# Sixteen shift numbers transposed at once and laid out as two rows by a DMA

## The chip, the cores and the metric

The kernel runs on one core of a Trainium2 chip. The metric is the device time of one execution, in microseconds (us). Five engines work side by side, each on its own program in order, and wait for one another on semaphores: TensorE (PE: matmuls, and PEld for loading its stationary operand), VectorE (DVE), ScalarE (ACT), GpSimd (POOL) and SyncE (SP), which here issues nearly all DMAs.

## The reference, cut to what matters

Two layers run one behind the other on eight sequences (the batches below) of 512 rows and 512 features: a graph attention, and then a transformer block. The change lies in the attention of the second. Shortened:

```
h = gamma * layernorm(hidden) + beta            # [8, 512, 512]
q, k, v = split(h @ Wqkv.T + bqkv)              # 16 heads of 32
energy = q @ k.T                                # per head [512, 512]
att = softmax(energy, axis=-1) / sqrt(512)
out = (att @ v) @ Wp.T + bp
h1 = out + hidden
y = gamma * layernorm(h1) + beta + h1
```

The softmax needs, for each query row, a number that is subtracted before the exponential: the row's maximum.

## The kernel before, in words

The function `attention` goes through 8 batches of 8 pairs of heads (`batch`, p from 0 to 7), 64 pairs in all. The heads' q and k are held as sums of a high and a low part, and are stacked for one matmul: `sq_stack` and `sk_stack` (`sq`, `sk`) have in rows 0 to 95 the three products' parts, and in rows 96 and 97 `sq` has the shift, in two parts (high and low), while `sk` has ones. So the matmul of 98 rows gives energy minus maximum at once.

For a pair, PE makes the energies twice. `scores` (L1351, 8 tiles of 128 queries by 512 keys, two heads by NT = 4 tiles) is for the maxima alone: DVE reduces each tile (`maximum`, L1167) into `mx`, and `shift_parts` (L1175, L1177) makes the 16 negated numbers per partition in `shift` (2 heads, 4 tiles, 2 parts). `shift_t` turns them from columns into rows on PE, by matmuls against the identity (L1359), into PSUM; ACT copies the rows into `sq` (`shift_rows`, L1058). `scores_t` (L1375) then makes the transposed energies with the shift, ACT takes the exponential (`exps`, L1067, into `pt`), and `weighted` multiplies with v and with ones (L1389, L1391).

This is staggered over pairs: while pair p goes through `scores_t`, `exps` and `weighted`, the `scores` of the next pair run between them, and `shift_t` of the next pair stands near the end of the pair. Behind it, and ahead of the next pair's `scores_t`, PE has filling work written out by hand: half a projection of 6 matmuls (L48 to L50) behind most pairs, 30 matmuls at p = 1, 18 at p = 4, and at p = 0 only the pair's last `weighted`. In the first and the last batch some of the filling is missing: p = 2 of the first and p = 4 of the last have only their `weighted` too. Where a pair has half a projection there, its last `weighted` is held back until behind the next pair's first `scores_t`.

SP issues the DMAs in the order of its own program: `stacks` copies a chunk of q and k (two pairs) from `qh`, `ql`, `kh`, `kl` into the stacks by 24 DMAs of 64 KB (L930), and stands at the head of each even p; `load_t` stands in p = 1, `store_y` and `load_h` in p = 7, where SP waits for the last piece of the batch before. A chunk's 24 DMAs are asked for one or two pairs before they are used. Batches 0, 1, 2 and 7 stand in the program by themselves; 3 to 6 are a loop of two passes with two batches each.

Below, T0 to T7 are the moments at which the `shift_t` *for* pair 0 to 7 of a batch begins (T0 falls in the pair p = 7 of the batch before, T1 in p = 0). The lag of a pair is the time from its T to its first `scores_t`.

Of the kernel before, what the change touches and what calls it, by code (L numbers as in the profile page):

```python
# [16 lines left out]
F32 = mybir.dt.float32  # L17
# [6 lines left out]
P = 128  # L24
# [789 lines left out]
def attention(nc, t, d):  # L814
# [12 lines left out]
    with ExitStack() as ctx:  # L827
        def sb(name, shape, dt=F32):
# [17 lines left out]
        mx = sb("mx2", [P, 2, NT, 2])  # L846
        shift = sb("shift", [P, NT, 2, 2], F32R)
# [5 lines left out]
                          "k_ready qh_done ql_done kh_done kl_done e_ready emax_done sh_hi sh_lo sh_ready shrow_done "  # L853
                          "et_ready exp_done pv_done den_done oraw_done rden_done o_done oh_done ol_done v_ready v_done "
                          "pj_ready hb_done h1_done st_done mv_done ve_done rstd_done nmr_done ln_done mulg_done "
                          "addb_done y_done y_out")
# [43 lines left out]
        def _(sp):  # L900
# [31 lines left out]

            def batch(b, bpar, more):
                for p in range(PAIRS):
                    c = p // 2
                    if p % 2 == 0 and (c < 3 or more):
                        stacks((c + 1) % FC, 4 * b + c + 2)
                    if p == 1 and more:
                        sp.wait_ge(s["hl_done"], 4 * b + 4)
                        load_t(b + 1)  # L940
                    if p == 7:
                        if first(b):
                            load_h(b)
                        else:
                            sp.wait_ge(s["y_done"], 4 * b)
                            store_y(b - 1)
                            load_h(b)

# [6 lines left out]
            stacks(0, 1)  # L955
            batches(sp, batch)
# [72 lines left out]
        def _(act):  # L1029
# [24 lines left out]
            def shift_rows(b, p):  # L1054

                for k in range(2):
                    act.wait_ge(s["sh_ready"], 2 * (PAIRS * b + p) + k + 1)
                    nc.scalar.activation(sq[3 * DH:3 * DH + 2, (p // 2) % 2, 2 * (p % 2) + k, :],  # L1058
                                         bank[3 * DH:3 * DH + 2, 2 + k, :], ACT.Copy).then_inc(s["shrow_done"], 1)
# [94 lines left out]
        def _(dve):  # L1154
# [8 lines left out]
            def maximum(b, p, i):  # L1163

                dve.wait_ge(s["e_ready"], 8 * (PAIRS * b + p) + i + 1)
                k, n = divmod(i, NT)
                nc.vector.reduce_max(mx[:, p % 2, n, k:k + 1], bank[:, 2 + i % 2, :], AX).then_inc(s["emax_done"], 1)  # L1167

            def shift_parts(b, p):

                G = PAIRS * b + p
                dve.wait_ge(s["emax_done"], 8 * G + 8)
                if not (isinstance(b, int) and G == 0):
                    dve.wait_ge(s["sh_ready"], 2 * G)
                nc.vector.tensor_scalar(shift[:, :, :, 0], mx[:, p % 2], -1.0, None, ALU.mult).then_inc(s["sh_hi"], 1)  # L1175
                dve.wait_ge(s["sh_hi"], G + 1)
                nc.vector.scalar_tensor_tensor(shift[:, :, :, 1], mx[:, p % 2], -1.0, shift[:, :, :, 0].bitcast(F32),  # L1177
                                               ALU.mult, ALU.subtract).then_inc(s["sh_lo"], 1)
# [112 lines left out]
        def _(pe):  # L1291
# [44 lines left out]
            def scores(b, p, i):  # L1336
# [3 lines left out]
                if i == 0:  # L1340
                    pe.wait_ge(stq[c % 2][p % 2], STK * (use(b, c) + 1))
                    pe.wait_ge(stk[c % 2][p % 2], STK * (use(b, c) + 1))
                    if not (isinstance(b, int) and G == 0):
                        pe.wait_ge(s["shrow_done"], 2 * G)
# [9 lines left out]
            def shift_t(b, p):  # L1354

                pe.wait_ge(s["sh_lo"], PAIRS * b + p + 1)
                for k in range(2):
                    for n in range(NT):
                        last = nc.tensor.matmul(bank[3 * DH:3 * DH + 2, 2 + k, n * P:(n + 1) * P],  # L1359
                                                shift[:, n, k, :].bitcast(F32), t["ident"][:, :],  # L1360
                                                start=True, stop=True)
                    last.then_inc(s["sh_ready"], 1)

            def scores_t(b, p, i):
# [3 lines left out]
                for k in range(2):  # L1368
                    if i == 0:
                        pe.wait_ge(s["shrow_done"], 2 * G + k + 1)  # L1370
# [230 lines left out]
```

## Time and profile before

| | |
|---|---|
| time before, median of 3 runs | 1713.22 us (1706.87 to 1714.64) |
| the profiled execution: span from the first to the last instruction | 1703.8 us |
| time of the profiled execution beside its span | the page states the span alone; the runs lie 3.1 to 10.8 us above it |
| PE busy | 1563.1 us, 92% |
| DVE, ACT, POOL busy | 58%, 43%, 23% |
| first and last `shift_t` | 636.8 and 1655.1 us |
| matmuls of `shift_t` | 1024 instructions, 125.1 us |
| ACT copies of the shift rows | 128, 75.5 us |

A busy share is an average over the span. What a change is worth is read from which wait ends last at its place.

### The profile page before, as it was taken

Reading aid. Unit: us, or ns where it says so; the run is one execution under the profiler, and the core shown is the slowest. Engines: PE = TensorE matmul, PEld = TensorE weight load, DVE = VectorE, ACT = ScalarE, POOL = GpSimd, SP = SyncE. Lnnn points to the kernel's source line nnn. Section 1 sums busy time; section 2 is a strip of 40 time slices with the busy share of each in tenths; the row PEclk is TensorE's granted clock in tenths of the full one; section 3 lists DMA queues with packets and bytes.
Section 4 is the critical chain, followed back from the end, with each engine's and each line's share of the span. In section 5 each row is a group of like instructions: output and inputs, shape, how many; then the busy total and the mean of one; then the engine's idle time right before and its main releaser. Section 6 shows DMA issues by size and latency. Waiting matters only on the chain.

```text
span 1703.8 us, 22572 instructions
## 1 busy us (share of the span) xinstructions
PE 1563.1 (92%) x7716; PEld 927.4 (54%) x7716; DVE 984.3 (58%) x1454; ACT 726.9 (43%) x1249; POOL 394.3 (23%) x265
## 2 busy tenths in 40 slices
PE   6979899999997279999999999999998999999993
PEld 4646566666665254555555555555554554654542
DVE  2533567666676335556556565665655666566665
ACT  0231334234341325554554554554454455465361
POOL 1023344333432040110140140140131131032032
PEclk9989999999998689999999999999999999999997
DMA  9454133342322432122133133133132124123112
GB/s 293 171 179 131 53 126 128 134 150 79 128 85 75 175 90 72 48 85 81 39 112 86 38 109 90 38 109 84 44 98 75 47 57 133 38 62 104 45 41 74
DMA packets 97180, 162.24 MB, mean 95 GB/s; under 512 B 39104, under 2 KB 47616, under 8 KB 90928
## 3 DMA queue, kind: packets, MB, share of 16 engines
q1 hardware_dynamic: 95920, 160.44, 30.6%
q8 instruction: 62, 1.02, 0.3%
q10 hardware_dynamic: 1152, 0.41, 0.1%
q14 instruction: 46, 0.38, 0.1%
HBM read 72.67 MB, written 37.78 MB: 65 GB/s over the span
## 4 chain that ended last, share of the span: by engine, by line
PE 58%; DVE 5%; issue 1%; ACT 1%; POOL 1%; DMA 1%; SPq 0%; DVEq 0%; ACTq 0%; POOLq 0%
PE a_bank L1389 13%; PE a_bank L1351 9%; PE a_bank L48 8%; PE a_bank L1359 7%; PE a_bank L49 7%; PE a_bank L50 7%; PE a_bank L1375 7%; DVE mx L1167 3%; DVE shift L1175 1%; PE a_bank L1391 1%; DMA traw<-t_rows 1%; POOL hl L968 0%; ACT pt L1067 0%; DVE o L1189 0%; DVE rden L1184 0%
## 5 line engine op out<-in xcount | busy, mean ns | idle before, releaser
L1167 DVE TENSOR_REDUCE mx<-a_bank 128x1 f32<-128x512 f32 x512 | 339.9, 687 | 256.6 <-PE a_bank L1351 252.1
L1067 ACT ACTIVATE pt<-a_bank 128x512 f32<-128x512 f32 x512 | 277.3, 595 | 151.4 <-PE a_bank L1375 148.3
L1391 PE MATMUL a_bank<-pt,ones 128*32 128x512 f32 x1024 | 276.3, 606 | 0.0
L1389 PE MATMUL a_bank<-pt,v 128*32 128x512 f32 x1024 | 272.3, 606 | 0.0
L1351 PE MATMUL a_bank<-sk_stack,sq_stack 96*128 96x512 f32 x512 | 206.9, 445 | 5.5 <-DVE mx L1167 2.1
L1351 PEld LDWEIGHTS a_bank<-sk_stack,sq_stack 96*128 96x128 f32 x512 | 88.0, 188 | 186.7 <-DVE mx L1167 135.0
L1375 PE MATMUL a_bank<-sq_stack,sk_stack 98*128 98x512 f32 x512 | 169.0, 406 | 2.5 <-ACT pt L1067 1.7
L1058 ACT ACTIVATE sq_stack<-a_bank 2x512 fp32r<-2x512 f32 x128 | 75.5, 590 | 206.4 <-PE a_bank L1359 206.4
L740 PE MATMUL g_bank<-m,sf 128*128 128x320 f32 x512 | 155.2, 446 | 1.9 <-issue 1.9
L1359 PE MATMUL a_bank<-ident,shift 128*2 128x128 f32 x1024 | 125.1, 276 | 13.2 <-DVE shift L1177 13.2
L48 PE MATMUL a_bank<-hh,wqkh 128*128 128x512 f32 x256 | 107.8, 421 | 25.8 <-POOL hl L968 25.0
L978 POOL TENSOR_TENSOR rstd<-ve,mhalf 128x4 f32<-128x4 f32 x8 | 8.1, 1018 | 495.3 <-DVE ve L1220 495.3
L1375 PEld LDWEIGHTS a_bank<-sq_stack,sk_stack 98*128 98x128 f32 x512 | 96.3, 190 | 44.0 <-ACT pt L1067 15.5
L1359 PEld LDWEIGHTS a_bank<-ident,shift 128*2 128x2 f32 x1024 | 82.8, 86 | 66.2 <-DVE shift L1177 34.9
L740 PEld LDWEIGHTS g_bank<-m,sf 128*128 128x128 f32 x512 | 93.4, 191 | 41.7 <-issue 11.1
L1184 DVE RECIPROCAL rden<-den 128x512 f32<-128x512 f32 x32 | 107.2, 3350 | 5.4 <-ACT den L1076 5.4
L49 PE MATMUL a_bank<-hl,wqkh 128*128 128x512 f32 x256 | 101.3, 396 | 0.0
L50 PE MATMUL a_bank<-hh,wqkl 128*128 128x512 f32 x256 | 100.9, 394 | 0.0
L1159 DVE SCALAR_TENSOR_TENSOR kl<-a_bank,bcol,kh 128x512 fp32r<-128x512 f32 x32 | 24.0, 750 | 115.6 <-ACT kh L1045 115.6
L48 PEld LDWEIGHTS a_bank<-hh,wqkh 128*128 128x128 f32 x256 | 48.6, 190 | 66.2 <-issue 58.3
L1389 PEld LDWEIGHTS a_bank<-pt,v 128*32 128x32 f32 x1024 | 39.1, 108 | 83.2 <-issue 78.4
L490 POOL TENSOR_TENSOR e<-e,cadd 128x640 f32<-128x640 f32 x32 | 49.5, 1547 | 130.1 <-DVE e L633 128.6
(164 smaller groups left out, 2606.2 us busy)
## 6 DMA issues: line engine op xcount, KB each, us to landing
sq_stack<-qh SPq DMA_DIRECT2D x256, 64.0 KB, 2.0
sk_stack<-kh SPq DMA_DIRECT2D x256, 64.0 KB, 2.0
m_rows<-mout SPq DMA_DIRECT2D x8, 1280.0 KB, 5.0
m<-m_rows SPq DMA_DIRECT2D x8, 1280.0 KB, 5.6
xraw<-in_x_t SPq DMA_DIRECT2D x8, 1024.0 KB, 7.7
xn<-in_x SPq DMA_DIRECT2D x8, 1024.0 KB, 5.0
h_rows<-xn SPq DMA_DIRECT2D x8, 1024.0 KB, 4.0
t_rows<-hout SPq DMA_DIRECT2D x8, 1024.0 KB, 3.9
```

Of the source, the lines that this page charges most:

```text
L48: nc.tensor.matmul(out, ah, bh, start=start, stop=False)
L49: nc.tensor.matmul(out, ah, bl, start=False, stop=False)
L50: return nc.tensor.matmul(out, al, bh, start=False, stop=stop)
L740: nc.tensor.matmul(out, sf2[:, par, f, i * P:(i + 1) * P], m[:, f, dr, :], start=f == 0, stop=False)
L1067: nc.scalar.activation(pt[:, i, k, :], bank[:, k, :], ACT.Exp).then_inc(s["exp_done"], 1)
L1167: nc.vector.reduce_max(mx[:, p % 2, n, k:k + 1], bank[:, 2 + i % 2, :], AX).then_inc(s["emax_done"], 1)
L1184: nc.vector.reciprocal(rden[:, :], den[:, :]).then_inc(s["rden_done"], 1)
L1351: nc.tensor.matmul(bank[:, 2 + i % 2, :], sq[0:3 * DH, c % 2, j, n * P:(n + 1) * P], sk[0:3 * DH, c % 2, j, :], start=True, stop=True).the ...
L1359: last = nc.tensor.matmul(bank[3 * DH:3 * DH + 2, 2 + k, n * P:(n + 1) * P], shift[:, n, k, :].bitcast(F32), t["ident"][:, :], start=True, ...
L1375: nc.tensor.matmul(bank[:, k, :], sk[0:3 * DH + 2, c % 2, j, i * P:(i + 1) * P], sq[0:3 * DH + 2, c % 2, j, :], start=True, stop=True).the ...
L1389: nc.tensor.matmul(bank[a:a + DH, 4 + p % 2, :], v[:, bpar, i, (2 * p + k) * DH:(2 * p + k + 1) * DH], w, start=i == 0, stop=i == NT - 1)
L1391: last = nc.tensor.matmul(bank[r:r + DH, 4 + p % 2, :], ones32[:, :], w, start=i == 0, stop=i == NT - 1)
```

## The change

`shift` is stored with part and head outermost, so that one transpose on PE turns the whole [128, 16] block into [16, 128] (one instruction instead of eight matmuls in the program). ACT copies these 16 short rows of 128 numbers from PSUM into a new SBUF tile `sht`. A DMA that SP issues then lays them out as the two rows of 2 x 512 numbers in `sq`. `scores_t` waits for that DMA (`shrow_in`), the next pair's `scores` for the copy (`sht_done`). On SP the new `shift_rows` stands at the end of each pair's piece of the program, behind `stacks`, `load_t` or `load_h`.

```
-        mx = sb("mx2", [P, 2, NT, 2])
-        shift = sb("shift", [P, NT, 2, 2], F32R)
+        mx = sb("mx2", [P, 2, 2, NT])
+        shift = sb("shift", [P, 2, 2, NT], F32R)
+        sht = sb("sht", [4 * NT, P])
...
         @block.sync
+            def shift_rows(b, p):
+                G = PAIRS * b + p
+                sp.wait_ge(s["sht_done"], G + 1)
+                sp.dma_start(sq[3 * DH:3 * DH + 2, (p // 2) % 2, 2 * (p % 2):2 * (p % 2) + 2, :].bitcast(F32)
+                             .rearrange("o k (n c) -> o (k n) c", c=P), sht[:, :]).then_inc(s["shrow_in"], 16)
...
                             load_h(b)
+                    if next_pair(b, p, more):
+                        shift_rows(*next_pair(b, p, more))
...
             sp.wait_ge(s["set_up"], 4)
             stacks(0, 1)
+            shift_rows(0, 0)
...
         @block.scalar
             def shift_rows(b, p):
-                for k in range(2):
-                    act.wait_ge(s["sh_ready"], 2 * (PAIRS * b + p) + k + 1)
-                    nc.scalar.activation(sq[3 * DH:3 * DH + 2, (p // 2) % 2, 2 * (p % 2) + k, :],
-                                         bank[3 * DH:3 * DH + 2, 2 + k, :], ACT.Copy).then_inc(s["shrow_done"], 1)
+                G = PAIRS * b + p
+                act.wait_ge(s["sh_ready"], G + 1)
+                if not (isinstance(b, int) and G == 0):
+                    act.wait_ge(s["shrow_in"], 16 * G)
+                nc.scalar.activation(sht[:, :], bank[0:4 * NT, 2, 0:P], ACT.Copy).then_inc(s["sht_done"], 1)
...
         @block.tensor
             def shift_t(b, p):
                 pe.wait_ge(s["sh_lo"], PAIRS * b + p + 1)
-                for k in range(2):
-                    for n in range(NT):
-                        last = nc.tensor.matmul(bank[3 * DH:3 * DH + 2, 2 + k, n * P:(n + 1) * P],
-                                                shift[:, n, k, :].bitcast(F32), t["ident"][:, :],
-                                                start=True, stop=True)
-                    last.then_inc(s["sh_ready"], 1)
+                nc.tensor.transpose(bank[0:4 * NT, 2, 0:P], shift[:, :, :, :].rearrange("p e k n -> p (e k n)").bitcast(F32),
+                                    t["ident"][:, :]).then_inc(s["sh_ready"], 1)
...
             def scores_t(b, p, i):
                     if i == 0:
-                        pe.wait_ge(s["shrow_done"], 2 * G + k + 1)
+                        pe.wait_ge(s["shrow_in"], 16 * G + 16)
                         pe.wait_ge(s["exp_done"], 8 * G)
```

In the program of SP, this is the end of one batch and the beginning of the next in the program before: the loads of p = 7 (L908, L909), the 24 DMAs of `stacks` of p = 0, `load_t` of p = 1 (L905), and the first of the next `stacks`.

```order
231 L908 DMA h<-h_rows 128x2048
232 L909 DMA rows<-gb_rows 128x1024
233 L930 DMA sq_stack<-qh 32x512 [waits qh_done]
234 L930 DMA sq_stack<-qh 32x512 x3
...
237 L930 DMA sk_stack<-kh 32x512 [waits kh_done]
238 L930 DMA sk_stack<-kh 32x512 x3
...
243 L930 DMA sk_stack<-kh 32x512 x4
244 L930 DMA sk_stack<-kl 32x512 x2
245 L905 DMA traw<-t_rows 128x2048 [waits hl_done]
246 L930 DMA sq_stack<-qh 32x512 [waits qh_done]
```

The same place in the changed program (its line numbers are one higher; L938 is the new DMA of the shift rows):

```order
237 L909 DMA h<-h_rows 128x2048
238 L910 DMA rows<-gb_rows 128x1024
239 L938 DMA sq_stack<-sht 2x8x128 [waits sht_done]
240 L931 DMA sq_stack<-qh 32x512 [waits qh_done]
241 L931 DMA sq_stack<-qh 32x512 x3
...
250 L931 DMA sk_stack<-kh 32x512 x4
251 L931 DMA sk_stack<-kl 32x512 x2
252 L938 DMA sq_stack<-sht 2x8x128 [waits sht_done]
253 L906 DMA traw<-t_rows 128x2048 [waits hl_done]
254 L938 DMA sq_stack<-sht 2x8x128 [waits sht_done]
255 L931 DMA sq_stack<-qh 32x512 [waits qh_done]
```

A shift DMA now stands on each side of the 24 DMAs: the one for pair 0 ahead of them and the one for pair 1 behind them. The first DMAs of the 24, which waited only for `qh_done`, now also come behind the wait for pair 0's copy.

In the program of PE, this is the end of pair 0 in the program before (the `shift_t` for pair 1):

```order
1008 L1389 MATMUL a_bank<-pt,v 32x512 [waits exp_done]
1009 L1391 MATMUL a_bank<-pt,ones 32x512
1010 L1389 MATMUL a_bank<-pt,v 32x512
1011 L1391 MATMUL a_bank<-pt,ones 32x512
1012 L1359 MATMUL a_bank<-ident,shift 2x128 [waits sh_lo]
1013 L1359 MATMUL a_bank<-ident,shift 2x128 x7
1014 L1389 MATMUL a_bank<-pt,v 32x512 [waits exp_done]
1015 L1391 MATMUL a_bank<-pt,ones 32x512
1016 L1389 MATMUL a_bank<-pt,v 32x512
```

In the changed program the eight are one:

```order
1009 L1397 MATMUL a_bank<-pt,v 32x512
1010 L1399 MATMUL a_bank<-pt,ones 32x512
1011 L1369 MATMUL a_bank<-ident,shift 16x128 [waits sh_lo]
1012 L1397 MATMUL a_bank<-pt,v 32x512 [waits exp_done]
1013 L1399 MATMUL a_bank<-pt,ones 32x512
```

Nothing else moves on PE. The work between this transpose and the next pair's `scores_t` is one `weighted`.

## Rows read from the trace of the kernel before

**Rows 1.** The page, part 1: busy time of each engine.

```profile
PE 1563.1 (92%) x7716; PEld 927.4 (54%) x7716; DVE 984.3 (58%) x1454; ACT 726.9 (43%) x1249; POOL 394.3 (23%) x265
```

**Rows 2.** The page, part 5: the shift's matmuls and copies.

```profile
L1058 ACT ACTIVATE sq_stack<-a_bank 2x512 fp32r<-2x512 f32 x128 | 75.5, 590 | 206.4 <-PE a_bank L1359 206.4
...
L1359 PE MATMUL a_bank<-ident,shift 128*2 128x128 f32 x1024 | 125.1, 276 | 13.2 <-DVE shift L1177 13.2
```

**Rows 3.** Chain that ended last, one batch: start, us, engine, line (T2 to T1).

```profile
915.23 1.84 PE a_bank L1359 x16
...
924.10 0.47 PE a_bank L1375 x2
...
936.75 1.84 PE a_bank L1359 x16
...
940.17 0.47 PE a_bank L1375 x2
...
952.80 1.84 PE a_bank L1359 x16
...
966.52 1.84 PE a_bank L1359 x16
...
972.71 0.47 PE a_bank L1375 x2
...
985.34 1.84 PE a_bank L1359 x16
...
1001.41 1.84 PE a_bank L1359 x16
...
1018.82 1.91 PE a_bank L1359 x16
...
1022.32 0.47 PE a_bank L1375 x2
...
1031.65 1.58 PE a_bank L1359 x13
...
1034.41 0.66 PE a_bank L1375 x2
```

**Rows 4.** View of line L790: one-instruction transposes, ns min/median/max.

```profile
L790 PE MATMUL g_bank<-ident,ln x128: 272/273/447, 232.3 to 576.6; 128*128 128x128 f32 x128
```

**Rows 5.** Groups by form, ACT: busy us, mean ns, idle before.

```profile
L161 ACT ACTIVATE mout<-p_bank 128x320 f32<-128x320 f32 x32 | 14.0, 437 | 50.8 <-PE p_bank L317 47.5 <-DMA m_rows<-mout 3.3
```

**Rows 6.** Timeline of SP's issues, around T2 and around T1.

```profile
909.61 2.41 SPq L930 DMA_DIRECT2D sq_stack<-qh  x4
912.06 1.23 SPq L930 DMA_DIRECT2D sq_stack<-ql  x2
919.50 2.42 SPq L930 DMA_DIRECT2D sk_stack<-kh  x4
...
930.76 1.23 SPq L930 DMA_DIRECT2D sk_stack<-kl  x2
...
1033.20 1.22 SPq L930 DMA_DIRECT2D sk_stack<-kl  x2
```

**Rows 7.** DMA view: queue's packets and share, issues with us to landing.

```profile
q1 hardware_dynamic: 95920, 160.44, 30.6%
...
sq_stack<-qh SPq DMA_DIRECT2D x256, 64.0 KB, 2.0
...
bcol<-in_bqkc SPq DMA_DIRECT2D x1, 6.0 KB, 1.6
```

**Rows 8.** Timeline of POOL and of DVE ahead of T0.

```profile
1013.95 4.58 POOL L973 TENSOR_TENSOR h<-h,bp 128x2048 f32<-128x2048 f32 x1 [7.68 <-DMA h<-h_rows]
...
1015.65 2.91 DVE L1175 TENSOR_SCALAR shift<-mx 128x8 fp32r<-128x8 f32 x1
```

**Rows 9.** Timeline of PE, and stretches (busy by engine, PEclk, DMA).

```profile
1283.57 3.21 PE L1359 MATMUL a_bank<-ident,shift 128*2 128x128 f32 x16 [2.79 <-DVE shift L1177]
...
1284.00:1287.00 3.00, 3.00 (x16) 1.81 (x15) 0.18 (x1) 0.77 (x2) 0.00 (x0) 0.62 0.03 5
```

More of the change, by code:

```diff
@@ L852, in attention @@
         s = sems(nc, ctx, "w_in0 w_in1 w_in2 w_in3 w_hi w_lo w_lo_pool ld_c t_in h_in rows_in stq00 stq01 stq10 stq11 stk00 stk01 stk10 stk11 set_up bv_done hh_done hl_done q_ready "
-                          "k_ready qh_done ql_done kh_done kl_done e_ready emax_done sh_hi sh_lo sh_ready shrow_done "
+                          "k_ready qh_done ql_done kh_done kl_done e_ready emax_done sh_hi sh_lo sh_ready "
                           "et_ready exp_done pv_done den_done oraw_done rden_done o_done oh_done ol_done v_ready v_done "
                           "pj_ready hb_done h1_done st_done mv_done ve_done rstd_done nmr_done ln_done mulg_done "
-                          "addb_done y_done y_out")
+                          "addb_done y_done y_out sht_done shrow_in")
         stq = ((s["stq00"], s["stq01"]), (s["stq10"], s["stq11"]))
@@ L1166, in maximum @@
                 k, n = divmod(i, NT)
-                nc.vector.reduce_max(mx[:, p % 2, n, k:k + 1], bank[:, 2 + i % 2, :], AX).then_inc(s["emax_done"], 1)
+                nc.vector.reduce_max(mx[:, p % 2, k, n:n + 1], bank[:, 2 + i % 2, :], AX).then_inc(s["emax_done"], 1)
             def shift_parts(b, p):
@@ L1173, in shift_parts @@
                 if not (isinstance(b, int) and G == 0):
-                    dve.wait_ge(s["sh_ready"], 2 * G)
-                nc.vector.tensor_scalar(shift[:, :, :, 0], mx[:, p % 2], -1.0, None, ALU.mult).then_inc(s["sh_hi"], 1)
+                    dve.wait_ge(s["sh_ready"], G)
+                nc.vector.tensor_scalar(shift[:, 0], mx[:, p % 2], -1.0, None, ALU.mult).then_inc(s["sh_hi"], 1)
                 dve.wait_ge(s["sh_hi"], G + 1)
-                nc.vector.scalar_tensor_tensor(shift[:, :, :, 1], mx[:, p % 2], -1.0, shift[:, :, :, 0].bitcast(F32),
+                nc.vector.scalar_tensor_tensor(shift[:, 1], mx[:, p % 2], -1.0, shift[:, 0].bitcast(F32),
                                                ALU.mult, ALU.subtract).then_inc(s["sh_lo"], 1)
@@ L1343, in scores @@
                     if not (isinstance(b, int) and G == 0):
-                        pe.wait_ge(s["shrow_done"], 2 * G)
+                        pe.wait_ge(s["sht_done"], G)
                 if i < 2:
```

## The prediction

> **What bounds the kernel now.** I read the page first, then the chain that ended last in one whole batch, then the timelines of SP and ACT beside it, and last the DMA view. PE is busy for 92% of the span [rows 1], and in the batch that I followed the chain runs through PE almost without a gap: the reader should see in [rows 3] that `shift_t` itself stands on the chain, 1.84 us for 16 instructions, with PE work directly behind it. So PE's time there is worth its full length, as long as nothing else takes its place as the last wait. The copies of the shift rows by ACT are 128 times 590 ns [rows 2]; they end before PE has done its filling work, and cost nothing.
>
> [Rows 3] give two kinds of numbers, which carry everything below. Lags (from T to the first `scores_t`): pair 2: 924.10 - 915.23 = 8.87; pair 3: 3.42; pair 5: 6.19; pair 0: 3.50; pair 1: 2.76. Pairs 4, 6 and 7 have pair 3's lag. Distances: T0 to T1 12.83, T4 to T5 13.72, T6 to T7 16.07, T7 to T0 17.41.
>
> **What is removed.** PE has 16 matmul instructions per pair at 1.84 / 16 = 0.115 us each. The new transpose is one instruction. The nearest row is the 128x128 transposes of the graph layer, 128 instructions of 273 ns for 128 transposes [rows 4]: one instruction each, the same length as one of the 1024. PE is thus free again after about 0.115 us instead of 1.84, 1.73 us sooner in each of 64 pairs, 110 us in all, if nothing took the place of the matmuls. The two DVE instructions and their order stay.
>
> **What is added: a longer path from T to the rows.** Until now ACT wrote the rows itself. Now:
> - transpose ends: 0.27 us after T [rows 4];
> - ACT copies 16 x 128. Not in the trace. 512 columns take 590 ns [rows 2], 320 take 437 [rows 5]: 0.8 ns per column, so 128 columns take about 437 - 192 x 0.8 = 283 ns; at most it is the 437 itself. I take 0.27;
> - SP issues the DMA as soon as it is told (0.02), if its queue is free;
> - from issue to landing: 64 KB between two SBUF tiles take 2.0 us, the shortest small one in the trace, 6 KB, 1.6 us [rows 7]. The new one carries 8 KB. I take 2.0, since it goes the same way as the stacks' DMAs, with 1.6 as the lower bound;
> - PE starts: 0.05.
>
> Together L = 2.61 us. The upper bound of the landing comes from how the DMA is cut. It has 16 source rows and 2 destination rows. The mean packet of the queue took 0.306 x 16 x 1703.8 / 95920 = 0.087 us [rows 7]. If only two of the 16 DMA engines share the 16 pieces, eight lie behind one another, where two do in a stack's DMA: 6 x 0.087 = 0.5 us more, 2.5 us.
>
> The Trainium skill, page "DMA: Bandwidth & Descriptors", section "Why a DMA increments its semaphore by 16 and not by 1", says that the number of DMA engines is the largest up to 16 that divides the slowest dimension of both sides; for 16 and 2 that would be two engines, so by that page the sum would be the longer one (the last rival), and by the row of the 64 KB DMA the shorter.
>
> With L = 2.61 the lags become:
> - Pair 2 (batches 1 to 7): 30 matmuls behind the transpose cover L fully. -1.73 x 7 = -12.1.
> - Pairs with half a projection behind them and a free queue: PE would be ready at 3.42 - 1.73 = 1.69, but waits until 2.61. Only -0.81 remains of 1.73. These are pair 3 (7 times), 4 (8), 6 (7), 0 (8) and pair 2 of the first batch: 31 x -0.81 = -25.1.
>
> **The queue is not free everywhere.** SP issues in order, and `shift_rows` for pair 1 and for pairs 5 and 7 stands behind 24 stack DMAs, which themselves now stand behind the shift DMA of the pair before. Six of them took 3.68 us when nothing was queued (0.613 each), and a run of 18 from 919.50 to 931.99, 12.49 us (0.694 each) [rows 6]. I take 0.65: 15.6 us for 24. The lower bound is 14.7, the upper 16.7. In the trace before, the same run ended at 1034.42, 2.77 us behind T1 [rows 3, 6], which hurt nobody, since nothing for pair 1 was queued behind it. Now the run starts at T + 0.56 (copy) + 0.5 (issue of the shift DMA, as one stack DMA) and ends at T + 16.66; the next shift lands at T + 18.7. K's first DMA comes at its turn at about T + 5, while the copy that it waits for was done before 919.50, that is before T2 + 4.3, and moves forward with PE; so no other wait moves in. Then:
> - Pair 1: T1 is at T0 + 12.83 - (3.50 - 2.61) = T0 + 11.94, so the lag is 18.7 - 11.94 = 6.8 instead of 2.76: +4.0. The same holds wherever the pair ahead is short and has a stack run: pair 3 of the first batch and pair 5 of the last. 10 x 4.0 = +40.
> - Pair 5 (batches 0 to 6): T5 is at T4 + 12.9, so the lag is 5.8 instead of 6.19: -0.4 x 7 = -2.8.
> - Pair 7: T7 is at T6 + 15.26, so the lag is 3.4, as before: 0. The distance from T7 to T0 has no gain to lose either; in five batches it is held by DVE's L1175, which took 2.91 us and ended with POOL's addition [rows 8].
> - Pairs 6 and 7 of the last batch (lag about 2.7 before): 0.
>
> Sum so far: -12.1 - 25.1 - 2.8 + 40 = 0.
>
> **The clock.** In those ten places PE stands still from about T1 + 1.1 (one `weighted`) to T1 + 6.8, 5.7 us. The trace has one wait of nearly that kind: PE idle 2.79 us ahead of T0 at 1283.57. The 16 matmuls behind it took 3.21 us, and the granted clock was 0.62 over the following 3 us, a mixture of 2.4 and 1.2 GHz [rows 9]. At the T0 of the followed batch PE had waited too, about 1.3 us (T7 to T0 is 17.41, T6 to T7 16.07), and its 16 matmuls took the usual 1.91 us [rows 3]. So the ten long stalls should each bring a stretch at 1.2 GHz. Its price by that row is 1.3 us (3.21 against 1.91), at most about double. I take 1.5: +15 us. The 31 waits of 0.9 us should bring none. What hides the stall of pair 1 is nothing: the `scores`, exponentials and maxima of the next pair all stand behind that `scores_t`.
>
> The profiled execution would thus get 15 us longer, from 1703.8 to about 1719 us of span. The runs shown lie 3.1 to 10.8 us above that span; I put the same 15 us on their median: **1728 us**.
>
> **The rivals.**
> - *Forecast: the gain is eaten by the DMA's latency, and the queue behind 24 stack DMAs with the clock makes it slower.* 1728 us, its own range 1716 to 1740. Chance 0.5.
> - *The same, but the clock holds.* The row for it is T0 of the followed batch. 1713 us, no change. Chance 0.15. Between the two lies all of my uncertainty on [rows 9], which is one occurrence.
> - *A short transfer: faster.* Landing 1.6, issue 0.35, stack DMAs at 0.613. L = 2.21: 31 x -1.21 = -37.5; pair 2 -12.1; the run ends at T + 15.6 and the rows land at T + 17.3: pair 1 lags 17.3 - 11.5 = 5.8, +3.0 x 10 = +30; pair 5 lags 4.8, -1.4 x 7 = -9.8; pair 7 gains 1.0 twice (elsewhere DVE's lock holds T0), the last two pairs 1.0. That is -32; with the clock -17: 1696 us. It decides for faster from a landing of about 1.25 us on by itself, or 1.6 with the faster queue. For it speaks the 6 KB row, against it that all 64 KB DMAs, on a quiet queue too, need 2.0 [rows 7]. Chance 0.15.
> - *A longer transfer.* Landing 2.5: L = 3.11, 31 x -0.31 = -9.6; -12.1 - 2.8 + 40, that is +15.5; with the clock +31: 1744 us. Chance 0.2. The page named above would make this the likelier cut; against it stands that a 2 KB piece and a 512 B piece need not take the same, and no row has the latter alone.
>
> Faster by over 0.5% (a bound of about 8.6 us, what a measurement of this kernel can just tell) takes the third rival and little of the others: 0.14. Within 0.5%: the second rival, and the lower part of the forecast's own range: 0.28. Slower: the rest of the forecast, and the fourth: 0.58. The range, 8 in 10, is 1700 to 1749.
>
> **What the profile after would show.** One transpose of about 0.27 us per pair; PE busy about 110 us less; a new wait of `scores_t` on the DMA `sq_stack<-sht`, about 0.9 us in some thirty pairs and 5 to 6 us in ten, at pair 1 of each batch above all; the shift DMA at pair 1 issued 4 us after ACT's copy, directly behind a stack DMA; PEclk below 1 after these. The forecast is wrong if the small DMA lands in clearly less than 1.6 us or more than 2.5, if the stack DMAs are issued faster when nothing interrupts them, or if pair 1's stall leaves the clock alone.

## The result and the profile after

The changed kernel took 1744.39 us (median of 4 runs, 1742.53 to 1744.90), the kernel before, with one run more than in the table above, 1710.05 us (4 runs, 1704.36 to 1714.64): a ratio of 1.019, 95% interval 1.016 to 1.023. The profiled execution took 1742.53 us, 1.8 us more than its span of 1740.7 us, which is 36.9 us longer than that of before.

The page, parts 1, 4 and 5 of the kernel after:

```profile
PE 1490.4 (86%) x6756; PEld 858.5 (49%) x6756; DVE 987.7 (57%) x1454; ACT 675.5 (39%) x1185; POOL 393.5 (23%) x265
...
PE 34%; SPq 21%; DMA 4%; DVE 3%; issue 2%; ACT 1%; POOL 1%; ACTq 0%; DVEq 0%; POOLq 0%
...
L1383 PE MATMUL a_bank<-sq_stack,sk_stack 98*128 98x512 f32 x512 | 184.0, 443 | 110.1 <-DMA sq_stack<-sht 105.2
...
L1071 ACT ACTIVATE sht<-a_bank 16x128 f32<-16x128 f32 x64 | 17.0, 266 | 138.6 <-PE a_bank L1369 138.6
```

The same parts of the page of before (`scores_t` is L1375 there):

```profile
PE 58%; DVE 5%; issue 1%; ACT 1%; POOL 1%; DMA 1%; SPq 0%; DVEq 0%; ACTq 0%; POOLq 0%
...
L1375 PE MATMUL a_bank<-sq_stack,sk_stack 98*128 98x512 f32 x512 | 169.0, 406 | 2.5 <-ACT pt L1067 1.7
```

The reader should see three things against these and [rows 1, 2]. PE has 960 instructions less and is busy 72.7 us less, so the removal is real. `scores_t` (L1383) has a new wait on the DMA of the shift rows, 105.2 us in all. And the chain that ended last, which ran through PE in [rows 3], now runs for 21% of the span through SP's queue (`SPq`): through the issuing of DMAs.

The view of the new transpose's line (ns min/median/max):

```profile
L1369 PE MATMUL a_bank<-ident,shift x64: 270/271/382, 637.0 to 1692.4; 128*16 128x128 f32 x64
```

The chain after, in the batch of [rows 3], at pair 3 (a free queue) and at pair 5 (behind 24 stack DMAs):

```profile
952.33 0.28 ACT sht L1071
952.62 1.94 DMA sq_stack<-sht
954.61 0.73 PE a_bank L1383 x2
...
983.75 0.59 SPq L931
984.38 1.93 DMA sq_stack<-sht
986.36 0.73 PE a_bank L1383 x2
```

At pair 3 the chain goes copy, transfer, matmul. At pair 5 it comes from a stack DMA being issued (L931), which has nothing to do with the shift: only the order of the queue holds it.

T1 of the same batch, which stands just ahead of [rows 3], in the timeline of PE:

```profile
910.95 0.28 PE L1369 MATMUL a_bank<-ident,shift 128*16 128x128 f32 x1 [0.22 <-DVE shift L1189]
...
918.35 1.22 PE L1383 MATMUL a_bank<-sq_stack,sk_stack 98*128 98x512 f32 x2 [6.13 <-DMA sq_stack<-sht]
```

and in that of SP:

```profile
899.51 0.66 SPq L938 DMA_DIRECT2D sq_stack<-sht  x1
900.21 2.46 SPq L931 DMA_DIRECT2D sq_stack<-qh  x4
...
915.06 1.22 SPq L931 DMA_DIRECT2D sk_stack<-kl  x2
916.33 0.67 SPq L938 DMA_DIRECT2D sq_stack<-sht  x1
```

ACT's copy had ended at 911.6, 0.66 us behind T1. The DMA was issued at 916.33, when the 24 stack DMAs (16.1 us from 900.21) were through, and the matmul began 2.02 us later. Four stretches there (busy time of PE, PEld, DVE, ACT, POOL, then PEclk, DMA share, GB/s):

```profile
912.00:918.00 6.00, 0.22 (x4) 0.00 (x0) 2.85 (x2) 0.00 (x0) 0.00 (x0) 0.87 0.37 89
918.00:921.00 3.00, 2.65 (x6) 1.74 (x6) 0.96 (x2) 1.75 (x4) 0.00 (x0) 0.50 0.92 328
921.00:924.00 3.00, 3.00 (x13) 1.00 (x13) 0.32 (x1) 2.22 (x4) 0.00 (x0) 0.63 0.05 22
924.00:927.00 3.00, 3.00 (x14) 2.19 (x12) 0.60 (x1) 0.75 (x2) 0.00 (x0) 1.00 0.00 0
```

PE stands still for 6 us, and then works at a granted clock of 0.50 (1.2 GHz) and a mixture of both levels, until it is whole again at 924.

**Where the 37 us are.** I took T and the first `scores_t` of all 64 pairs from the timelines of PE of both kernels. That cuts the attention into 64 lags and 63 runs (a run goes from a pair's first `scores_t` to the next T). The last `scores_t` begins 38.7 us later than before: lags +2.1, runs +36.4, and 0.2 at the start.

| | lags, forecast | lags, measured | runs behind, measured |
|---|---|---|---|
| pair 2 | -12.1 and -0.8 | -13.6 | -0.5 |
| pairs 3, 4, 6, 0 (without pair 3 of the first batch) | -24.3 | -22.2 | +6.0 |
| pair 5 (batches 0 to 6) | -2.8 | +0.1 | +4.9 |
| pair 1 | +32 | +29.2 | +14.3 |
| pair 3 of the first, 5 of the last batch | +8 | +3.7, +4.8 | +1.5, +1.3 |
| pair 7 | 0 | 0.0 | +9.0 |

So the lags come to nothing, as the forecast had them. The whole loss is in the runs, in which the program is the same as before.

### The profile page after: what moved, and what is told of

Read it like the earlier page. It is cut to its first block, busy times and chain, and to the rows that moved or that the text cites. A ratio compares the mean times of both kernels' runs of the same rounds, so it can differ in the third digit from the quotient of the medians.

```text
span 1740.7 us, 20657 instructions
## 1 busy us (share of the span) xinstructions
PE 1490.4 (86%) x6756; PEld 858.5 (49%) x6756; DVE 987.7 (57%) x1454; ACT 675.5 (39%) x1185; POOL 393.5 (23%) x265
## 4 chain that ended last, share of the span: by engine, by line
PE 34%; SPq 21%; DMA 4%; DVE 3%; issue 2%; ACT 1%; POOL 1%; ACTq 0%; DVEq 0%; POOLq 0%
SPq L931 20%; PE a_bank L1397 9%; PE a_bank L1363 6%; PE a_bank L1383 5%; PE a_bank L48 5%; PE a_bank L49 4%; PE a_bank L50 4%; DMA sq_stack<-sht 4%; DVE shift L1187 1%; DVE mx L1179 1%; SPq L938 1%; DMA traw<-t_rows 1%; ACT sht L1071 1%; POOL hl L979 0%; PE a_bank L1369 0%
## 5 line engine op out<-in xcount | busy, mean ns | idle before, releaser
L1397 PE MATMUL a_bank<-pt,v 128*32 128x512 f32 x1024 | 289.2, 642 | 0.0
L1399 PE MATMUL a_bank<-pt,ones 128*32 128x512 f32 x1024 | 289.2, 642 | 0.0
L1383 PE MATMUL a_bank<-sq_stack,sk_stack 98*128 98x512 f32 x512 | 184.0, 443 | 110.1 <-DMA sq_stack<-sht 105.2
L1363 PE MATMUL a_bank<-sk_stack,sq_stack 96*128 96x512 f32 x512 | 216.3, 464 | 5.2 <-DVE mx L1179 2.0
L1363 PEld LDWEIGHTS a_bank<-sk_stack,sq_stack 96*128 96x128 f32 x512 | 92.9, 198 | 197.1 <-DVE mx L1179 127.2
L1383 PEld LDWEIGHTS a_bank<-sq_stack,sk_stack 98*128 98x128 f32 x512 | 100.3, 206 | 163.7 <-DMA sq_stack<-sht 133.9
L996 POOL TENSOR_TENSOR ln<-ln,rows 128x512 f32<-128x512 f32 x28 | 37.9, 1355 | 182.9 <-ACT ln L1103 182.9
L979 POOL TENSOR_TENSOR hl<-traw,hh 128x512 fp32r<-128x512 f32 x32 | 43.3, 1373 | 140.1 <-ACT hh L1046 140.1
L1071 ACT ACTIVATE sht<-a_bank 16x128 f32<-16x128 f32 x64 | 17.0, 266 | 138.6 <-PE a_bank L1369 138.6
L541 ACT ACTIVATE ln<-xn,nmr,rstd 128x512 f32<-128x512 f32 x32 | 23.4, 802 | 115.1 <-DVE nmr L685 115.1
```

Source lines behind the costliest of these rows:

```text
L1363: nc.tensor.matmul(bank[:, 2 + i % 2, :], sq[0:3 * DH, c % 2, j, n * P:(n + 1) * P], sk[0:3 * DH, c % 2, j, :], start=True, stop=True).the ...
L1383: nc.tensor.matmul(bank[:, k, :], sk[0:3 * DH + 2, c % 2, j, i * P:(i + 1) * P], sq[0:3 * DH + 2, c % 2, j, :], start=True, stop=True).the ...
L1397: nc.tensor.matmul(bank[a:a + DH, 4 + p % 2, :], v[:, bpar, i, (2 * p + k) * DH:(2 * p + k + 1) * DH], w, start=i == 0, stop=i == NT - 1)
L1399: last = nc.tensor.matmul(bank[r:r + DH, 4 + p % 2, :], ones32[:, :], w, start=i == 0, stop=i == NT - 1)
```

## Theories and experiments

**Theory 1** is the forecast's, with an addition from the profile: the removed matmuls are worth their full time, but (a) the shift DMA behind 24 stack DMAs makes PE wait some 6 us in ten places, (b) the clock behind these waits costs some 15 us, and (c) ahead of T0, DVE's L1187 waits for POOL's addition, now in six batches instead of five, +9 us. **Rival 2**: the detour through the DMA costs what it costs, in whatever queue it is issued, since every pair waits for it. **Rival 3**: the removed matmuls were worth little, since something else would have ended last. **Rival 4**: the clock falls because PE works less altogether, and not because of the waits at pair 1.

The first four kernels below were run beside the kernel before at 1710.92 us (median of 7 runs).

**The DMA in ACT's own queue.** ACT issues it directly behind its copy; SP's `shift_rows` is gone.

```diff
             def shift_rows(b, p):      # block.scalar
...
                 nc.scalar.activation(sht[:, :], bank[0:4 * NT, 2, 0:P], ACT.Copy).then_inc(s["sht_done"], 1)
+                act.wait_ge(s["sht_done"], G + 1)
+                act.dma_start(sq[3 * DH:3 * DH + 2, ...], sht[:, :]).then_inc(s["shrow_in"], 16)
```

> The changed kernel, but ACT issues the shift DMA itself, right behind its copy, so that it lies behind none of SP's stack DMAs. Theory 1 (the loss is the place behind the 24 stack DMAs, and what the clock adds behind those long waits): the lag of pair 1 falls from 6.5 to 7.4 us to about 2.7, that of pairs 5 and 7 to 4.5 and 2.7, and the granted clock stays whole in the attention. Against the kernel before, the lags then sum to about -56 us (31 x -0.8, 7 x -1.8, 7 x -1.7, 7 x -0.8); up to 14 us are lost again where DVE waits for POOL ahead of T0: 1655 to 1670 us. Rival (the latency of a small DMA as such is what costs): no faster than the kernel before, 1710 or more. Rival (issuing on ACT delays the exponentials by 0.6 us a pair): 1690 to 1700.

Measured: 1657.33 us (1655.17 to 1665.12), ratio 0.969 (0.966 to 0.973). The timeline of PE and of ACT's queue at the last T1 of [rows 3]:

```profile
1020.99 0.28 PE L1362 MATMUL a_bank<-ident,shift 128*16 128x128 f32 x1 [0.22 <-DVE shift L1182]
...
1021.69 0.63 ACTq L1063 DMA_DIRECT2D sq_stack<-sht  x1
...
1023.68 0.73 PE L1376 MATMUL a_bank<-sq_stack,sk_stack 98*128 98x512 f32 x2 [1.41 <-DMA sq_stack<-sht]
```

The lag of pair 1 is 2.69 us here (2.57 to 2.85 in all batches), while SP is still issuing the last of its 24. Against the kernel before, all lags together lose 51.5 us, and the runs gain 1.6. Rival 2 falls: nothing but the queue, and with it the engine that issues, was changed, and the change became a gain of 3%. Rivals 3 and 4 fall with it, since the transposes are the same here. Theory 1 stands; the runs to T0 cost 2.9 us each in the first two batches also here.

**The same in SP's queue, but between the halves of the 24.** Where 24 stack DMAs stand ahead of the shift DMA, it is put behind the first twelve.

```diff
             def stacks(c, n, between=None):
                 for half in range(2):
+                    if half and between:
+                        shift_rows(*between)
...
```

> The changed kernel, but SP issues the shift DMA of pairs 1, 3, 5 and 7 between the two halves of a chunk's stack DMAs (behind the first 12) and no longer behind all 24. Nothing moves to another engine. Theory 1: the first half ends at T + 9, before the next copy is there, so no shift DMA finds the queue busy: about the same as with the DMA on ACT's queue, 1655 to 1670 us, pair 1's lag about 2.7. Rival (the second half now comes too late for the next scores, or for the next projection): PE waits on stack DMAs instead, 1700 or more.

Measured: 1668.30 us (1666.84 to 1671.53), ratio 0.974 (0.972 to 0.977). Pair 1's lag is 2.66 us. What is left against the run before is at T0, in the timeline of PE:

```profile
1007.71 0.27 PE L1371 MATMUL a_bank<-ident,shift 128*16 128x128 f32 x1
...
1011.55 0.72 PE L1385 MATMUL a_bank<-sq_stack,sk_stack 98*128 98x512 f32 x2 [2.18 <-DMA sq_stack<-sht]
```

The lag is 3.84 us: SP issued this DMA at 1008.31, 0.60 us behind T0, but it landed only 3.2 us later. Ahead of it in the same queue are the batch's store and loads (L909 and its neighbours), whose data were still moving. In six batches it landed only 2.8 to 3.4 us behind its issue; PE waited 1.8 to 2.3 us in five of them, and 3.7 in one, where the view names another end of the wait than the DMA. In some of them, not in the one shown, the clock falls behind it: the runs behind pairs 0 and 1 are 17.2 us longer in all than before, where they are 1.6 longer with ACT's queue. That is not shown to be the queue's doing: with ACT's queue the load of `h` had landed at least 0.3 us before T0, and the smaller load behind it by about the time of the shift DMA's issue. The one shift DMA that did meet these loads in ACT's queue (pair 7 of the first batch, issued 1.6 us behind the load of `h`) took 4.8 us.

**What the removed matmuls are worth by themselves.** The kernel before, with two of the eight matmuls of `shift_t` (four instructions of the sixteen). Three quarters of the shifts are left out; the exponential's argument is scaled by 1e-3, so that it stays in bounds.

```diff
-                    for n in range(NT):      # shift_t
+                    for n in range(1):
...
-                    nc.scalar.activation(pt[:, i, k, :], bank[:, k, :], ACT.Exp)
+                    nc.scalar.activation(pt[:, i, k, :], bank[:, k, :], ACT.Exp, scale=1e-3)
```

> The kernel before with two of the eight shift matmuls per pair and the ACT copies as they were, no DMA (it leaves out three quarters of the shift rows, and scales the exponent by a thousandth so that nothing overflows). It takes 12 x 0.115 = 1.38 us from PE in each of 64 pairs and adds no latency. Theory 1 (PE's time there is worth its full length): 64 x 1.38 = 88 us less, minus some 7 us where T0 is held by DVE and POOL: about 1630 us. Rival (something else is right behind PE, so the matmuls were worth less than they take): 1670 to 1710 us.

Measured: 1630.82 us (1628.24 to 1632.49), ratio 0.952 (0.949 to 0.954). All lags but two are 1.31 us shorter, 84.4 us in all, and the runs take 7.6 back: 2.7 ahead of T0, 3.0 behind pair 0, the rest at pairs 3 and 5. So the 1.73 us per pair of the forecast were worth their length, and the 110 us were really there to be had (without what the DMA takes). Rival 3 falls also by this.

**Filling pair 1's wait.** Matmuls whose result nobody reads stand behind the last `weighted` of p = 0, 15 of them, in the changed kernel. They add work, but leave lag and queue alone; a second version has 21 (`range(7)`).

```diff
+                    if p == 0:
+                        pe.wait_ge(s["ql_done"], 4 * b + 2)
+                        for f in range(5):
+                            mm3(nc, bank[:, 6, :], ..., hh[:, 0, :], hl[:, 0, :], True, True)
```

> The changed kernel with 15 extra matmuls of 512 columns (about 3.5 us, results unused) at the end of p = 0, inside PE's wait of 5 to 6 us for pair 1's rows. Nothing is waited for sooner or later by it. Theory 1 (the clock costs 1.5 us or a little more behind each of these waits): the granted clock stays whole behind T1, the run from pair 1's first scores_t to T2 is again 12.5 us instead of 14, so 8 x 1.5 to 1.8 = 12 to 14 us less than the changed kernel: about 1731 us. Rival (those 14 us are not the clock's, but come from engines that start again in step): 1744 us, no change.

Measured: 1738.46 us (1732.83 to 1743.01), ratio 1.014 (1.011 to 1.017). A miss, and it did not settle the question: 1.5 to 2.5 us of the wait were left in seven batches, the clock fell behind them all the same, and the runs behind pair 1 were 15.0 us longer than before, as in the changed kernel. In the eighth 0.7 us were left, and the run there was as short as before.

This second version, the two with another DVE instruction and the first early transpose (both below) ran beside the kernel before at 1712.85 us (14 runs).

> The changed kernel with 21 extra matmuls instead of 15 at the end of p = 0 (4.8 us of PE's wait of 5.3 us). With 15 the granted clock still fell behind T1, after a rest of about 2.5 us. Theory 1 (what the pair behind the wait loses is the clock's): with the rest of the wait under 1.5 us the clock stays whole there, and the run from pair 1's first scores_t to T2 is 12.5 us again, 8 x 1.5 to 2 us less than the changed kernel: about 1731 us. Rival (the run stays at 14 us with a whole clock): 1744 us.

Measured: 1728.54 us (1720.64 to 1732.47), ratio 1.009 (1.006 to 1.012). The timeline of PE and the stretches there:

```profile
1049.34 0.74 PE L1383 MATMUL a_bank<-sq_stack,sk_stack 98*128 98x512 f32 x2 [0.89 <-DMA sq_stack<-sht]
```

```profile
1049.00:1052.00 3.00, 2.66 (x14) 1.21 (x14) 1.29 (x2) 2.12 (x5) 0.00 (x0) 1.00 0.86 289
1052.00:1055.00 3.00, 3.00 (x19) 2.15 (x12) 0.00 (x0) 1.74 (x4) 0.00 (x0) 1.00 0.14 60
```

The lag is as long as ever (the lags of pair 1 are +34.2 us here, +29.2 in the changed kernel), but PE works in it, the clock is whole behind it, and the runs behind pair 1 are -0.7 us instead of +14.3. That is (b), measured: 15.0 us for eight places, 1.9 each. The times alone would not show it so cleanly: the runs to T0 are also 8 us shorter in this kernel, and pair 7's lags 3.3 longer, since everything there is shifted in time.

**T0 and POOL's addition.** First what the changed kernel does there, in the timelines of POOL, DVE and PE:

```profile
1030.15 4.53 POOL L984 TENSOR_TENSOR h<-h,bp 128x2048 f32<-128x2048 f32 x1 [9.10 <-DMA h<-h_rows]
```

```profile
1030.17 4.54 DVE L1187 TENSOR_SCALAR shift<-mx 128x8 fp32r<-128x8 f32 x1
1034.75 0.17 DVE L1189 SCALAR_TENSOR_TENSOR shift<-mx,shift 128x8 fp32r<-128x8 f32 x1
```

```profile
1034.97 0.28 PE L1369 MATMUL a_bank<-ident,shift 128*16 128x128 f32 x1 [2.98 <-DVE shift L1189]
```

DVE's instruction on 8 numbers per partition began with POOL's and ended with it: 4.54 us instead of 0.17. PE waits 2.98 us. [Rows 8] shows the same with 2.91 us. My first idea was that the kind of DVE instruction matters, and that one that reads two operands would pass:

```diff
-                nc.vector.tensor_scalar(shift[:, 0], mx[:, p % 2], -1.0, None, ALU.mult)
+                nc.vector.scalar_tensor_tensor(shift[:, 0], mx[:, p % 2], -2.0, mx[:, p % 2], ALU.mult, ALU.add)
```

> The changed kernel with DVE's first shift instruction made of another kind (scalar_tensor_tensor, mx * -2 + mx, the same numbers, instead of tensor_scalar with -1). In the trace of the changed kernel, tensor_scalar ahead of T0 took 4.5 us and ended with POOL's addition of bp. Theory 1a (tensor_scalar alone of the two waits while POOL works, and the runs from pair 7 to T0 lost 9 us more than before by that): the instruction takes 0.2 us in every pair, the run from pair 7 to T0 falls to 12.7 us in all batches, 9 us plus the 9 us that the kernel before loses there too: 1726 us. Rival (the second shift instruction waits in its place, or PE was waiting there for something else): 1744 us.

Measured: 1744.74 us (1743.59 to 1745.30), ratio 1.019 (1.016 to 1.021). A miss; the idea fell:

```profile
1031.33 0.17 DVE L1187 SCALAR_TENSOR_TENSOR shift<-mx 128x8 fp32r<-128x8 f32 x1
1031.53 4.49 DVE L1189 SCALAR_TENSOR_TENSOR shift<-mx,shift 128x8 fp32r<-128x8 f32 x1
```

Here the first instruction was through before POOL began (1031.48), and the second waited 4.49 us. In three other batches the exchanged first instruction itself took 4.0 to 4.2 us. The Trainium skill, page "SBUF — State Buffer", section "Who interferes with whom", says that a VectorE instruction with two inputs in SBUF contends with a GpSimd instruction that reads SBUF, and that one waits for the other to end; this trace agrees with 4.49 us. The same edit was made in the kernel before (with its order of `shift`):

> The kernel before with the same exchange of DVE's first shift instruction. Theory 1a: T7 to T0 becomes 16.1 us in all batches, where five of them had 17.5 to 18.9: 9 us less than before, 1702 us. Rival: no change, 1711 us.

Measured: 1707.14 us (10 runs, 1700.24 to 1714.39), ratio 0.996 (0.994 to 0.998); T7 to T0 is 17.59 us there, so this rather went with the rival of its expectation. A gain of 0.4% (0.2 to 0.6), on whose place I found nothing.

What can be moved is POOL's addition. It needs nothing that is urgent, so it is made to wait for DVE's two instructions for pair 0, in both kernels:

```diff
                         if p == 0:      # POOL's program
+                            pool.wait_ge(s["sh_lo"], PAIRS * b + 1)
                             add_bp(b - 1)
```

> The changed kernel, but POOL's addition of bp (4.6 us, once per batch) waits until DVE's shift instructions for pair 0 are done. Exchanging the kind of the DVE instruction did not help: the other kind took 4.2 us there too. Theory 1b (any DVE instruction with its operands in SBUF waits while this addition runs, whatever its kind; T0 is late because POOL's addition begins just ahead of it): the shift instruction takes 0.2 us in every pair, the run from pair 7's scores_t to T0 is 12.8 us in all batches (9 us were added by the change, and 9 were there before): about 18 us less than the changed kernel, 1726 us. Rival (the addition now disturbs DVE's work behind T0 as much): 1744 us.

Measured: 1727.57 us (1726.86 to 1731.62), ratio 1.012 (1.007 to 1.017). Beside it, beside its counterpart below and beside the last two kernels of all, the kernel before took 1709.79 us (12 runs).

```profile
1032.23 0.17 DVE L1188 TENSOR_SCALAR shift<-mx 128x8 fp32r<-128x8 f32 x1
...
1032.78 4.92 POOL L984 TENSOR_TENSOR h<-h,bp 128x2048 f32<-128x2048 f32 x1 [9.68 <-DVE shift L1190]
```

The runs to T0 are 5.8 us shorter than in the kernel before, where they had been 9.0 longer: 14.8 us for one line. A hit in time, but not in every batch: five runs to T0 are 12.7 to 12.8 us, as forecast, and in the first two, where the clock fell behind a wait of pair 7, they are 14.3. That L1187 waits for POOL's addition is shown. How much of the change's own loss that is depends on the next run.

> The kernel before with the same wait for POOL. Theory 1b: the five late T0 go back to 16.1 us behind T7: 9 us less, about 1702 us. Rival: no change, 1711 us.

Measured: 1694.70 us (9 runs, 1693.50 to 1696.67), ratio 0.990 (0.988 to 0.993). More than forecast. The runs to T0 are 9.0 us shorter, and the lags and runs of pair 0 another 2.5: the kernel before had been paying for the collision too. With the addition moved in both, the changed kernel is still 32.9 us slower (1727.57 against 1694.70), where it had been 34.3 slower; the profiled spans differ by 31.9 us instead of 36.9. So moving the addition is worth 15 to 17 us in either kernel, and the collision explains only 1 to 5 us of the difference between them. The kernel before spread from 1701.91 to 1718.61, these runs over 3.2 us, so part of its spread may be the chance of where POOL's addition falls; that is only argued.

**Can the DMA be hidden?** With ACT's queue, each pair without long filling still waits about 0.9 us. So `shift_t` goes ahead of both halves of the projection instead of between them.

```diff
+                    if nxt:
+                        shift_t(*nxt)
                     for part in (PART1, PART2):
...
-                        if part == PART1 and nxt:
-                            shift_t(*nxt)
```

> As act_queue, and the transpose stands ahead of both halves of the half projection (12 matmuls) instead of between them. act_queue still waits about 0.9 us for the DMA in most pairs. Theory 1 (of the saved 1.73 us per pair the uncovered latency took 0.9): 6 more matmuls, 1.4 us, cover it; PE waits 0.1 to 0.3 us for DVE instead. About 30 x 0.7 = 20 us less than act_queue: 1635 to 1640 us. Rival (the wait for DVE takes the place of the DMA's, since the maxima end only just in time): 1655 us.

Measured: 1654.20 us (1649.66 to 1660.98), ratio 0.967 (0.963 to 0.970). A miss: the time can't be told from that of ACT's queue alone (0.966 to 0.973). The wait for the DMA is gone where it was aimed at, but at pairs 2, 5, 6 and 7 PE now waits 1.1 to 1.3 us for DVE's last maxima before the transpose. Against ACT's queue alone, the run up to the transpose and the lag of pairs 3, 4 and 0 together became 0.8 to 1.2 us shorter in most batches, those of 2 and 5 1.3 to 1.5 longer, and those of 6 and 7 stayed the same within 0.2. So it pays only where DVE is ahead of PE, which is at pairs 3, 4 and 0:

```diff
+                    early = p in (2, 3, 7)
+                    if early and nxt:
+                        shift_t(*nxt)
...
-                        if part == PART1 and nxt:
+                        if part == PART1 and nxt and not early:
```

> As act_queue, with the transpose ahead of both halves of the filling work in p = 2, 3 and 7 alone (the shifts for pairs 3, 4 and 0), and between the halves elsewhere. In act_early these three gained 0.9 to 1.0 us each against act_queue, pairs 2 and 5 lost 1.3 each to DVE's maxima, 6 and 7 nothing. Theory 1 (in each pair the later of DMA and maxima decides, pair by pair): about 22 x 0.9 = 20 us less than act_queue, 1637 us. Rival (the waits only move to the pairs behind): 1655 us.

Measured: 1648.75 us (1644.30 to 1655.98), ratio 0.965 (0.959 to 0.970). Missed: it is not clear of ACT's queue alone either. In three batches PE, now earlier still, meets POOL's addition at T0 (waits of 3.6 to 4.1 us), and the clock falls behind it. With `pool.wait_ge` as above added:

> early_where_short and POOL's later addition together. If both effects add: 1637 - 6 to 9 (T0 is late in fewer batches there, since PE comes sooner than POOL's addition in some) = 1629 us. Rival (no further gain from POOL, since the collision had gone already): 1637 us.

Measured: 1631.24 us (1629.69 to 1634.08), ratio 0.955 (0.950 to 0.960). It beats both kernels: 4.5% under the one before, 6.5% under the changed one (1631.24 / 1744.39). Its page, part 4, and the view of waits (in all, times, longest):

```profile
PE 51%; DVE 6%; DMA 4%; issue 1%; ACT 1%; POOL 1%; SPq 0%; ACTq 0%; DVEq 0%; POOLq 0%
```

```profile
PE a_bank L1377 <- DMA sq_stack<-sht: 36.6, 27, 4.4
```

SP's queue is off the chain, and the wait for the shift DMA has shrunk from 105.2 us to 36.6.

## Why the prediction was right or wrong

The forecast was slower, for the reason of the queue and the clock behind it, and that is what happened; 1744 lies in the range. The size was off: +15 us was forecast on the profiled execution's span, +36.9 came, and +34.3 on the medians. Some half of that is in terms that the sum had at nothing. That 1744 is also the number of the rival with a longer transfer is chance: the transfer took what the forecast said.

- **What is removed**: right. The new transpose takes 271 ns like those of [rows 4], and 1.73 us per pair came free, and a little more, where nothing new was waited for: pair 2's lag fell by 1.82 in batches 1 to 7. "PE busy about 110 us less" did not come: it was 72.7. The same matmuls took longer (those of `weighted` 642 ns on average instead of 606), at a mean granted clock of 0.941 instead of 0.968.
- **L = 2.61**: right. The copy took 0.27, was done 0.57 to 0.67 us behind T (0.75 the first time), and the lags of pairs 3, 4, 6 and 0 behind a free queue are 2.53 to 2.72, but for pair 0 of two batches (2.85 and 3.72). The landing took 1.9 to 2.0 us from the issue, like that of 64 KB, so the rival with 2.5 fell. The number of engines may still be the two of the Trainium skill's page "DMA: Bandwidth & Descriptors" (section "Why a DMA increments its semaphore by 16 and not by 1"): in the trace the semaphore of this DMA steps three times per transfer, the last two times within 0.02 us of one another (at the T0 of [rows 8], 1.92 and 1.93 us behind the issue), and that of a stack DMA 16 times. What fell is the price of 0.5 us that the forecast had put on two engines. The rival with 1.6 fell too.
- **The queue behind the stacks**: right. The run of 24 took 16.1 us against 15.6, and the lag of pair 1 behind them 7.40 against 6.8, the longest of the eight (from 4.39). The issue of the shift DMA was put at 0.5 "as one stack DMA", though [rows 6] give 0.61 to 0.69 for one; it took 0.61 to 0.71. The sum over eight batches is +29.2 against +32, since T1 came late in two of them (+2.35 and +1.69 instead of 3.8 to 4.7). Pair 5's lags are 5.5 to 6.6 us against 5.8, so its sum is +0.1 instead of -2.8.
- **"The clock. 10 x 1.5 = +15"**: right in place and size. The ten runs behind these waits are 14.3 + 1.5 + 1.3 = +17.1 us, and filling eight of the waits took 15.0 away.
- **"The distance from T7 to T0 has no gain to lose either"**: this step failed: the sum had it at nothing, and the runs to T0 are 9.0 us longer, the largest error. I took L1175's wait for POOL as a fixed floor. But it ends when POOL's addition ends, and both can move. At the T0 of [rows 8] DVE had arrived 1.7 us behind POOL's start and waited 2.91 us; now it arrives with the start and waits for the whole, 4.54. One batch that had been free of the wait now has it, 3.32 us. Together these are 3.7 us. In the last four batches (+5.3 us) DVE waits no longer than before (2.8 to 3.3 us against 3.0 to 4.3), but both came later behind pair 7's first `scores_t`: POOL's start by 0.1 to 1.9 us, since the loads landed later (below), and DVE by 1.5 to 1.6, since the clock fell behind pair 7's waits of 1.6 to 1.7 us. The T0 one batch later, first before and then now, in the timelines of POOL and DVE:

```profile
1145.71 4.57 POOL L973 TENSOR_TENSOR h<-h,bp 128x2048 f32<-128x2048 f32 x1 [7.87 <-DMA h<-h_rows]
...
1147.36 2.95 DVE L1175 TENSOR_SCALAR shift<-mx 128x8 fp32r<-128x8 f32 x1
```

```profile
1165.39 4.56 POOL L984 TENSOR_TENSOR h<-h,bp 128x2048 f32<-128x2048 f32 x1 [9.69 <-DMA h<-h_rows]
...
1166.66 3.32 DVE L1187 TENSOR_SCALAR shift<-mx 128x8 fp32r<-128x8 f32 x1
```

Pair 7's first `scores_t` began at 1136.28 and 1154.04. Moving POOL took 14.8 us away from these runs, but 9.0 in the kernel before too: by the two medians and the two spans only 1 to 5 us are the change's by way of the collision.

- **"The 31 waits of 0.9 us should bring none"**: right for these. What I did not price are the waits between 1 and 2.5 us. Pair 5's had been forecast (it says nothing of its clock), and in three of seven batches the clock fell behind them, 1.6 us each, +4.8. In the last batch the run behind pair 6 is 4.3 longer: a wait of 1.29 us at 1679.27, then the clock, and at its end a wait of 1.77 us for DVE, whose two shift instructions took 0.71 and 1.18 us there while POOL was at work on tiles of 128 x 512 (L996 to L1000); before, they took 0.19 and 0.17. Pair 7's waits of 1.6 to 1.7 us belong here too, as said above.

Stretches at pair 5 of the followed batch, and at pair 6 of the last one:

```profile
983.00:986.00 3.00, 1.64 (x8) 1.03 (x6) 1.20 (x3) 0.60 (x1) 0.00 (x0) 1.00 0.35 87
986.00:989.00 3.00, 2.64 (x12) 1.27 (x13) 0.17 (x1) 1.69 (x3) 0.00 (x0) 0.85 0.00 0
989.00:992.00 3.00, 3.00 (x12) 0.82 (x11) 1.12 (x2) 2.21 (x4) 0.00 (x0) 0.59 0.00 0
```

```profile
1678.00:1681.00 3.00, 1.70 (x5) 0.86 (x5) 1.10 (x3) 1.08 (x2) 2.86 (x3) 1.00 0.01 3
1681.00:1684.00 3.00, 3.00 (x11) 0.89 (x11) 0.57 (x1) 2.37 (x4) 1.17 (x1) 0.50 0.00 0
1684.00:1687.00 3.00, 3.00 (x13) 1.26 (x12) 1.98 (x3) 1.66 (x3) 0.00 (x0) 0.50 0.03 5
```

Both read alike: a stretch with PE busy for little over half, and then, while PE is busy throughout, a granted clock of 0.59 in one and 0.50 in the other. The missing 21.9 us (36.9 less 15) are thus T0's 9.0, pair 5's 4.8, the last batch's 4.3, the lags' 2.1 and the ten places' other 2.1, 22.3 in all; the rest about cancels. These are places and not causes: at T0 POOL's addition, the later loads and the clock go together, and no run took all three apart.

Still open: `load_h` landed 8.5 us after its issue (median) where it had taken about 7.2 before, which sets when POOL's addition starts, and so the collision. No run separated it. What makes the clock fall behind one wait of 1.7 us and not behind the next was not tried either.

## What to carry to other kernels

When work moves from an engine to a DMA, price the queue before the transfer: here the 2 us of the transfer ate half the gain at most pairs, and 4 us behind DMAs that nobody was waiting for, ten times, ate the rest; an otherwise quiet queue turned +1.9% into -3.1%. Treat a wait for another engine's long instruction not as a floor but as a function of when both arrive: shift each by 1 us, and look at what is met. Move such an instruction in the kernel before as well, or its gain is put down to the change. And where an idle gap ahead of matmuls grows to between one and a few microseconds, allow for what the matmuls behind it cost at 1.2 GHz: in these runs 1.3 to 1.6 us behind some of the waits of 1.3 to 2.5 us, and 1.9 us on average behind the long ones of pair 1.

## What the runs showed of the hardware that I had not expected

- The clock fell behind waits much shorter than [rows 9] had led me to think: 1.29 us (last batch) and 1.72 us (followed batch). But a wait's length does not decide it: at pair 5, waits of 1.85 and 1.71 us in two other batches left the clock alone, as did one of 2.49 us at pair 5 in the kernel with 21 filling matmuls. With ACT's queue, pair 1 waited 1.41 us in the batch of [rows 3]'s last T1 and 1.42 us three batches later. The first brought these stretches, and a run 1.30 us longer, the second a run as long as ever:

```profile
1023.00:1026.00 3.00, 2.32 (x6) 1.17 (x6) 2.96 (x4) 1.79 (x4) 0.00 (x0) 0.83 0.79 225
1026.00:1029.00 3.00, 3.00 (x13) 1.13 (x13) 0.19 (x1) 2.06 (x4) 0.00 (x0) 0.60 0.36 153
```

- A DVE instruction of 0.17 us took up to 4.54 us beside POOL's addition of 128 x 2048 numbers in SBUF, one with a single tensor input (4.54) like one with two (4.49).
- 8 KB from 16 rows into 2 rows took 1.9 to 2.0 us from issue to landing on a quiet queue, and 1.9 to 2.2 with stack DMAs from another queue in flight. While the loads of a batch were moving ahead of it in its own queue it took 2.8 to 3.4 us. In ACT's queue it took 4.2 to 5.3 us in the six cases (one or two in each of the four kernels that issue it there) in which SP had issued a load of 1 MB within the 1.6 us before it, or the 0.3 us behind it.
